# Rotary halves of the key units: exchanged by ScalarE out of PSUM in place of a DMA

## The reference

```python
def rotate_half(x):
    x1, x2 = jnp.split(x, 2, axis=-1)
    return jnp.concatenate((-x2, x1), axis=-1)
def apply_rope(x):
    ...
    return (x * jnp.cos(phase) + rotate_half(x) * jnp.sin(phase)).astype(x.dtype)
q = apply_rope((layernorm(x) @ Wq).reshape(b, t, 32, 128))
k = apply_rope((ctx @ Wk).reshape(b, t, 8, 128))
v = (ctx @ Wv).reshape(b, t, 8, 128)
weights = softmax(where(mask, 30 * tanh(0.0884 * q k / 30), -1e30))
x = x + (weights @ v) @ Wo
gate, up = layernorm(x) @ dq(w1).T, layernorm(x) @ dq(w2).T   # dq: NF4, blocks of 64
x = x + (silu(gate) * up) @ dq(w3).T
```

## Time and profile before

| | us |
|---|---|
| median of 3 runs | 882.83 |
| the runs | 882.04, 882.83, 887.17 |
| the profiled execution | 888.34 |
| its span, first to last instruction | 886.5 |
| PE busy | 815.5 (92%) |
| DVE busy | 684.7 (77%) |
| POOL busy | 484.2 (55%) |
| ACT busy | 464.8 (52%) |

### The profile page before, as it was taken

One profiled execution on the slowest core, in us unless ns is written; L12 is line 12 of the kernel. 1 busy time (PEld: TensorE's weight loads), 2 busy tenths in 40 slices (PEclk: granted clock), 3 DMA queues, 4 the chain that ended last, 5 costly groups with the idle time before them and its releaser, 6 DMA issues.

```text
span 886.5 us, 10685 instructions
## 1 busy us (share of the span) xinstructions
PE 815.5 (92%) x3806; PEld 647.4 (73%) x3806; DVE 684.7 (77%) x745; ACT 464.8 (52%) x571; POOL 484.2 (55%) x270
## 2 busy tenths in 40 slices
PE   6798998899899899998999999989779999996898
PEld 4577886688677677776778777767567788885786
DVE  3886853887988789897989989968789889985220
ACT  5025842664766566637647656544544658576100
POOL 2555055675977669769879779683212134432100
PEclk9999999999999999999999999989989999998899
DMA  9667556233343433433434424214003113111210
GB/s 318 187 189 202 167 137 199 72 84 84 109 111 85 135 84 96 126 85 81 139 83 112 132 66 154 72 36 131 30 1 126 36 48 113 48 56 37 74 60 36
DMA packets 63541, 91.76 MB, mean 104 GB/s; under 512 B 6784, under 2 KB 30464, under 8 KB 63488
## 3 DMA queue, kind: packets, MB, share of 16 engines
q1 hardware_dynamic: 62304, 88.25, 34.5%
q10 hardware_dynamic: 1184, 2.82, 0.9%
HBM read 51.00 MB, written 19.07 MB: 79 GB/s over the span
## 4 chain that ended last, share of the span: by engine, by line
PE 54%; DVE 20%; POOL 10%; issue 7%; DMA 5%; ACT 3%; SPq 1%; DVEq 0%; POOLq 0%; ACTq 0%
PE bank L473 5%; PE bank L475 5%; PE bank L474 5%; POOL qT L1169 4%; PE bank L507 4%; PE bank L509 4%; PE bank L508 4%; PE bank L553 3%; PE avp L581 3%; DVE nfv L908 3%; PE bank L493 3%; PE bank L491 3%; PE bank L492 3%; PE trp L480 3%; DVE nfx L908 3%
## 5 line engine op out<-in xcount | busy, mean ns | idle before, releaser
L1226 POOL TENSOR_TENSOR eb<-eb,maskf 128x512 f32<-128x512 f32 x64 | 106.7, 1667 | 53.8 <-ACT eb L782 53.7
L780 ACT ACTIVATE eb<-bank 128x512 f32<-128x512 f32 x64 | 38.1, 595 | 155.8 <-PE bank L553 155.8
L1169 POOL TENSOR_TENSOR qT<-cs_loop,sw 128x512 f32<-128x512 f32 x58 | 90.7, 1564 | 49.2 <-DMA sw<-cs_loop 47.2
L507 PE MATMUL bank<-woh,ath 128*128 128x512 f32 x256 | 110.0, 430 | 0.0
L491 PE MATMUL bank<-xh,wqh 128*128 128x512 f32 x256 | 106.4, 416 | 0.0
L509 PE MATMUL bank<-woh,atl 128*128 128x512 f32 x256 | 103.1, 403 | 0.0
L508 PE MATMUL bank<-wol,ath 128*128 128x512 f32 x256 | 103.0, 402 | 0.0
L493 PE MATMUL bank<-xh,wql 128*128 128x512 f32 x256 | 101.3, 396 | 0.0
L492 PE MATMUL bank<-xl,wqh 128*128 128x512 f32 x256 | 101.1, 395 | 0.0
L716 ACT ACTIVATE nfq<-nfv,bnd 128x1408 uint8<-128x1408 f32 x60 | 84.9, 1461 | 19.7 <-POOL nfv L1185 19.7
L908 DVE SCALAR_TENSOR_TENSOR nfa<-nfq,nfa 128x1408 f32<-128x1408 uint8 x42 | 88.4, 2104 | 0.8
(11 more groups left out here) (140 smaller groups left out, 1960.9 us busy)
## 6 DMA issues: line engine op xcount, KB each, us to landing
sw<-cs_loop SPq DMA_DIRECT2D x116, 128.0 KB, 2.3
stage<-wq_pieces SPq DMA_DIRECT2D x32, 256.0 KB, 2.9
stage<-wo_pieces SPq DMA_DIRECT2D x32, 256.0 KB, 3.0
stage<-dq_scratch SPq DMA_DIRECT2D x32, 256.0 KB, 3.7
sw<-cs_start SPq DMA_DIRECT2D x44, 128.0 KB, 2.4
ks_scratch<-qT SPq DMA_DIRECT2D x16, 256.0 KB, 2.5
vs_scratch<-vst SPq DMA_DIRECT2D x16, 256.0 KB, 2.6
kcur<-ks_scratch SPq DMA_DIRECT2D x16, 256.0 KB, 2.9
```

The costliest lines, as they stand in the source:

```text
L507: nc.tensor.matmul(o, ah, wh[:, g, :], start=g == 0, stop=False)
L1169: nc.gpsimd.tensor_tensor(dst, products(ru, slot)[:, 0, :], sw[:, slot, :], ALU.add).then_inc(roped, 1)
L1226: nc.gpsimd.tensor_tensor(part, part, maskf[:, :].rearrange("p (o t) -> p o t", o=1).to_broadcast([128, G, S]), ALU.mult).then_inc(weights ...
```

## The change

For the key units alone:

- ScalarE copies the two halves of the bank out of PSUM into `sw`, exchanged, by two instructions on 64 partitions each (`key_swap`). It waits for the unit on TensorE and, by `cs_done`, until the slot of `sw` has been read.
- VectorE makes two products of 128x512 (`key_cos`, from the bank, and `key_sin`, from `sw`). It waits for `key_swapped` in place of `proj_done`. The sine product's sign no longer fits the table (the exchange comes before the product and not behind it), so that
- GpSimd subtracts where it added (`key_rope`), and waits for `cs_done` alone.
- SyncE's `swap` of the key units is gone.
- On ScalarE the copies of unit 0 stand behind the high part 11, the high parts 12 and 13 behind them, then the copies of unit 1, and the high parts 14 and 15 and the load of `nfv`. From unit 10 on the copies of a unit stand ahead of its `first_token_hi`.

```diff
@@ SyncE
             for u in range(NK):
-                swap(u, u % 2)
                 if u > 0:
                     k_store(u - 1)
@@ ScalarE
+            def key_swap(u):
+
+                act.wait_ge(proj_done, u + 1)
+                wait(act, cs_done, u - 1)
+                nc.scalar.activation(sw[0:64, u % 2, :], prj[u % 2][64:128, :], ACT.Copy)
+                nc.scalar.activation(sw[64:128, u % 2, :], prj[u % 2][0:64, :], ACT.Copy).then_inc(key_swapped, 1)
+
-            for n in range(16):
+            for n in range(12):
                 first_hi(n)
                 if n == 9:
                     act.dma_start(y[:, :, :], x_d.rearrange("b s d -> s b d")).then_inc(x_in, 16)
-            act.dma_start(nfv[:, :], nf_d[:, 0:CH]).then_inc(nf_in, 16)
-            for u in range(10, NK):
-                first_token_hi(u - 10)
+            for u in range(NK):
+                key_swap(u)
+                if u < 2:
+                    first_hi(2 * u + 12)
+                    first_hi(2 * u + 13)
+                if u == 1:
+                    act.dma_start(nfv[:, :], nf_d[:, 0:CH]).then_inc(nf_in, 16)
+                if u >= 10:
+                    first_token_hi(u - 10)
                 if u >= 12:
                     first_hi(u + 4)
@@ VectorE
+            def key_cos(u):
+
+                dve.wait_ge(key_swapped, u + 1)
+                wait(dve, roped, u - 1)
+                nc.vector.tensor_tensor(products(u, u % 2)[:, 0, :].rearrange("p (b t) -> p b t", b=4),
+                                        prj[u % 2][:, :].rearrange("p (b t) -> p b t", b=4),
+                                        tab[:, 0, :].rearrange("p (o t) -> p o t", o=1).to_broadcast([128, 4, S]),
+                                        ALU.mult)
+
+            def key_sin(u):
+
+                nc.vector.tensor_tensor(products(u, u % 2)[:, 1, :].rearrange("p (b t) -> p b t", b=4),
+                                        sw[:, u % 2, :].rearrange("p (b t) -> p b t", b=4),
+                                        tab[:, 1, :].rearrange("p (o t) -> p o t", o=1).to_broadcast([128, 4, S]),
+                                        ALU.mult).then_inc(cs_done, 1)
+
             for u in range(NK):
-                rope_parts(u, u % 2, tab[:, 0:2, :])
+                key_cos(u)
+                key_sin(u)
@@ GpSimd
+            def key_rope(u, dst):
+
+                pool.wait_ge(cs_done, u + 1)
+                part = products(u, u % 2)
+                nc.gpsimd.tensor_tensor(dst, part[:, 0, :], part[:, 1, :], ALU.subtract).then_inc(roped, 1)
+
-                rope(u, u % 2, qT[:, u % 8 // 4, u % 4, :])
+                key_rope(u, qT[:, u % 8 // 4, u % 4, :])
```

More of the change, by code:

```diff
@@ L172, in build @@
                                                     sem("h_lo"))
-        mask_step = sem("mask_step")
+        mask_step, key_swapped = sem("mask_step"), sem("key_swapped")
         down_done, final_done, stored = sem("down_done"), sem("final_done"), sem("stored")
@@ L1167, in rope @@
                 pool.wait_ge(cs_done, ru + 1)
-                pool.wait_ge(swapped[slot], 32 * (ru // 2 + 1))
+                pool.wait_ge(swapped[slot], 32 * ((ru - NK) // 2 + 1))
                 nc.gpsimd.tensor_tensor(dst, products(ru, slot)[:, 0, :], sw[:, slot, :], ALU.add).then_inc(roped, 1)
+            def key_rope(u, dst):
+                pool.wait_ge(cs_done, u + 1)
+                part = products(u, u % 2)
+                nc.gpsimd.tensor_tensor(dst, part[:, 0, :], part[:, 1, :], ALU.subtract).then_inc(roped, 1)
             def first_low(n):
```

## The result

The changed kernel takes 893.91 us in the median of 4 runs (891.14 to 895.85), the kernel before 882.46 (4 runs): ratio 1.0115, interval 1.0067 to 1.0163. Measured again (e1_again, 9 runs against 32) it is 1.0069, interval 1.0046 to 1.0092, or +6.1 us; the medians of these runs, 894.07 and 885.68, are 8.4 us apart. Single runs of one kernel on one chip spread over 7 to 12 us (before: 880.45 to 888.04 beside e1_again, 881.40 to 892.97 beside e9_ln_later), so that the sharper measure of the change is a place in the profile: the first value unit, behind which all goes on in one order. It starts at 76.99 us instead of 69.87: **+7.1 us**, 0.8% of the time, which lies in both intervals.

The account below looks back on a forecast made before the run. TensorE was taken as the bound, with 11.7 us open in the key stage and delays there arriving whole. Terms 2.7 + 1.8 - 1.3 + 2.3 + 1.4 - 0.8 = +6.1 on 882.83 gave 888.9 us, range 881 to 896.

Parts of the forecast that it names:

- Start: Key stage: unit 1 starts at 16.7 us instead of 13.97, behind unit 0's copies, products and a low part; +2.7 us.
- Clock at unit 1: After TensorE stands 4.8 us, most of a low-clock stretch at 1.2 GHz follows; +1.8 us, bounds 0 and 2.3.
- Unit 1 to the statistics: From unit 1's start to the layernorm's first statistics: 19.5 us instead of 20.8, blocking by GpSimd included; -1.3 us.
- Layernorm: From first statistics to unit 8's product: VectorE held by GpSimd's power and by two sums; +2.3 us.
- the sine product of unit 7 standing for the power: In the layernorm, unit 7's sine product on VectorE is held 1.1 us by GpSimd's power.
- Units 10 to 15 and the end: Last token copy stands behind ScalarE's copies (+0.5), low parts and normalised rows behind GpSimd's sums (+0.9); +1.4 us.
- rival B: Clock falls again at the gap before unit 10, and longer copies or a tight last round: 891.9 us; 0.20 with C.
- the 0.8 that I took off for the lateness of the layout: The layout puts the kernel before's first value unit at 70.7 us instead of 69.87; -0.8 us.
- the "few" sine products of 1.2 to 2 us: Sign in the profile: most sine products near 0.68 us, a few of 1.2 to 2, each beside a GpSimd op.
- A: Key stage without notable blocking or low clock: slightly faster, -1.2 us, 881.6 us; range -2 to +2, chance 0.16.
- The test that I gave it: A's deciding point: with blocking below about 1.5 us in the whole key stage, the change is not slower.
- C: Late context pieces on ScalarE hold the copies of the next unit; at most 1 us, inside B, chance 0.20 together.

Follow-up runs that it names:

- e9_ln_later: As e7, with the layernorm's small operations and two normalised blocks behind unit 8's products; ratio 0.9948 to the kernel before, first value unit at 65.99 us.
- e4: Changed kernel plus 16 matmuls of no use behind unit 0; ratio 1.0072 to the kernel before, first value unit at 75.58 us.
- e10: As e9_ln_later, with ScalarE's copies of unit 15 behind the last token copy and high part 19; ratio 0.9936 to the kernel before, 880.67 us.
- e3: Changed kernel with the exchanged halves written into PSUM, not SBUF; ratio 1.0034 to the kernel before, first value unit at 74.51 us.
- e2: Changed kernel with the low parts of units 0 to 5 ahead of the products on VectorE; ratio 1.0013 to the kernel before.
- e8: Changed kernel with one 128x512 copy in place of two of 64x512, halves not exchanged; ratio 1.0056 to the kernel before.
- e6: Changed kernel with the edits of e2 and e3 together: low parts first, halves in PSUM; ratio 0.9999 to the kernel before.
- e7: As e6, with ScalarE copying unit 0 ahead of weight parts 10 and 11; ratio 0.9981 to the kernel before.
- e5: Kernel before (exchange by DMA) with the low parts of units 0 to 5 ahead of the unit's product; ratio 0.9981 to the kernel before.
- e11: Kernel before (exchange by DMA) with low parts first and the layernorm's small operations behind unit 8; ratio 0.9980 to the kernel before.

## Why the prediction was right, and where its sizes were off

The forecast was +6.1 us, the key stage gave +7.1, and the two measurements of the time +6.1 and, with few runs, +10.1. That one of them meets the forecast to the tenth is chance: the medians of the same runs are 8.4 us apart. The mechanism held as a whole: the loss lies in the key stage, mostly at its start, and arrives at the first value unit (75 to 77 us forecast, 76.99 measured). By its terms, measured as the prediction defined them:

1. *Start:* +2.7 forecast, 17.32 - 13.97 = +3.35. The pair of copies takes 1.2 us and not 1.1: two copies of 0.59 us are 0.60 apart and don't overlap. Most of the rest is a weight part that landed 0.4 us later.
2. *Clock at unit 1:* +1.8 forecast (its own working, 4 x 0.43, gives 1.7); the unit took 5.5 us from first start to last end instead of 3.0, +2.4, just over the bound of 2.3 for a whole unit at the low level. e4 shows the cause: a shorter gap, a shorter low stretch, and the mark earlier by about as much. One thing stays unexplained: unit 0 starts with matmuls 0.43 us apart in both kernels, in windows whose granted clock reads 1.00, so at the start of the kernel the clock row doesn't tell the pace.
3. *Unit 1 to the statistics:* -1.3 forecast. 38.49 - 17.32 - 2.4 = 18.7 against 20.8: -2.1. Less of the blocking came through to TensorE than I reckoned: the two held low parts lost 1.10 us each and two sine products 0.64 together.
4. *Layernorm:* +2.3 forecast, 51.01 - 38.49 = 12.5 against 11.4: +1.1. The step that failed is the sine product of unit 7 standing for the power; it ran beside it (45.92, 0.68 us), so 1.1 us of the term weren't there. The second held small operation came as foretold.
5. *Units 10 to 15 and the end:* +1.4 forecast, 76.99 - 51.01 = 26.0 against 23.7: +2.3. 1.5 of them are rival B's low clock at unit 10; without it the term would be 0.8. e10 puts ScalarE's last copies at 0.35 (I had 0.5).

The measured terms make 3.35 + 2.4 - 2.1 + 1.1 + 2.3 = 7.1, without the 0.8 that I took off for the lateness of the layout. Term 3 came out lower than laid out by the same 0.8; if the lateness lay there, the two are one, but no run shows where it lay. So the sum is partly luck: the start, the clock at unit 1 and term 5 came out 2.2 us larger than forecast, and terms 3 and 4 made up for 2.0. Of the signs that I had named, unit 1's slow matmuls, the small operations held twice, the product of unit 8 at 51.01 and the first value unit came as said; of the "few" sine products of 1.2 to 2 us there is one, of 1.18.

Of the rivals, A is out by its number: it had -1.2 us, and -2 to +2 as its range. The test that I gave it fails too. I had written it as if all hung on the sine product, which is held for just 0.8 us in all, below A's 1.5, and still the change is slower: the start and the clock at unit 1 alone are 5.8 us. e3, which frees the sine product, brings unit 10 forward by 0.45 us. What stands longer than before, the second small operation, the mask operation and the normalised blocks, is held by GpSimd's sums because these now come right behind the products, and that e3 leaves as it is. B came true in its first half: gaps of 1.48 us before unit 9 and 2.69 before unit 10 (2.8 forecast for both), and a low clock at unit 10; its second half didn't come, since without the clock term 5 is 0.8. C didn't come either: ScalarE took the context pieces without a wait for a DMA between the copies, and unit 1's copies waited for TensorE (6.5 us).

What stays open is why the clock fell at unit 10 in the kernels that copy to SBUF (the changed kernel twice, e2, e4, e8) and not in those that copy to PSUM (e3, e6, e7), with the same gap of 2.7 us; nothing that I ran tells that apart from chance. Copies to PSUM are no shelter as such: e6 has a low stretch at unit 2 (0.79 in the window from 16 to 24 us), behind a gap of 2.36 us.

## What to carry to other kernels

When a step moves from a DMA to an engine, look at what is queued behind it on every engine that now waits: here a low part of 0.6 us behind the new wait cost some 5 us, and moving it ahead gave them back (5.5 by the mark, e2). A gap of TensorE costs more than its length when a low clock follows it, so close the first gap before you shorten anything else. And removing a latency pays only once what stands around it fits. Against the DMA with the same order of low parts (e5), the mark was 2.4 us later with copies to SBUF (e2), 0.15 earlier with copies to PSUM (e6) and 1.9 earlier with unit 0's copies ahead of two weight parts as well (e7); with the layernorm's order changed for both it was 2.65 us earlier (e9 against e11). The 2.4 and the 2.65 hold some 1.5 us of low clock each.

## What the runs showed of the hardware

- ScalarE copies 64 partitions to the other 64, out of PSUM, in 0.59 us for 512 columns, 0.57 into PSUM: as long as 128 partitions without a shift (0.60). Two such copies start 0.60 us apart and so don't overlap, and the next operation starts 0.61 behind the second. Behind e8's whole copies out of the same banks it mostly starts 0.50 later, and behind the second half copy into PSUM (e3) 0.50 too.
- GpSimd's power on 8 elements (1.64 us) didn't hold a VectorE product with two SBUF inputs that started inside it, in any of the five profiles that have this (0.68 us each). GpSimd's sums and low parts of 128x512 held such operations down to 8 elements (1.21 and 1.25 us), and not these alone: a `tensor_scalar` with one large SBUF input was held too (1.19 us instead of 0.54; in e9 one on 8 elements, 1.15 instead of 0.17). A `tensor_scalar` out of PSUM, started inside a sum of the kernel before, took its usual 0.28.
- It works the other way too. GpSimd's sum behind a running low part took 1.65 us instead of 1.28 (timeline of GpSimd, changed kernel):
```profile
16.65 1.65 POOL L1204 TENSOR_TENSOR qT<-cs_start 128x512 f32<-128x512 f32 x1 [5.19 <-DVE cs_start L945]
...
52.44 1.29 POOL L1204 TENSOR_TENSOR qT<-cs_start 128x512 f32<-128x512 f32 x1 [2.82 <-DVE cs_start L945]
```
